# Turning and adding split rows by DMA instead of TensorE and VectorE, in a graph network with a final layer norm

## The reference

```python
x = _layernorm(x + _L0_gnn_ref(x, adj, ...), axis=-1)      # graph convolution, two linear layers, two batch norms
x = _layernorm(x + _L1_gnn_ref(x, adj, ...), axis=-1)
# the last part of _L1_gnn_ref, h is [128 batches, 128 times, 128 channels]:
for p in range(1, 5):
    nw = Tv // p
    wins = h[:, :nw * p, :].reshape(Bv * nw, p, Hd)        # windows of p times
    last = _lstm_last(Wih[p-1], Whh[p-1], bih[p-1], bhh[p-1], wins)   # p steps of an LSTM, the last hidden state
    h = h.at[:, arange(nw) * p + (p - 1), :].set(last.reshape(Bv, nw, Hd))
```

## Time and profile before

| | us |
|---|---|
| median of 3 runs (756.95 to 757.46) | 757.35 |
| the profiled execution | 757.01 |
| its span in the trace | 755.2 |
| TensorE busy | 737.3 (98%) |
| VectorE busy | 657.6 (87%) |
| ScalarE busy | 538.8 (71%) |
| GpSimd busy | 316.5 (42%) |

### The profile page before, as it was taken

One profiled execution on the slowest core, in us unless ns is written; L12 is line 12 of the kernel. 1 busy time (PEld: TensorE's weight loads), 2 busy tenths in 40 slices (PEclk: granted clock), 3 DMA queues, 4 the chain that ended last, 5 costly groups with the idle time before them and its releaser, 6 DMA issues.

```text
span 755.2 us, 11504 instructions
## 1 busy us (share of the span) xinstructions
PE 737.3 (98%) x4016; PEld 426.6 (56%) x4016; DVE 657.6 (87%) x1391; ACT 538.8 (71%) x872; POOL 316.5 (42%) x287
## 2 busy tenths in 40 slices
PE   8999999999999999998999999999999999999994
PEld 6777644677777777673444444444444444554542
DVE  6888787888998989858998799889999898899987
ACT  4877898467777686659887686786676767666662
POOL 1000000159788887800000001600981946239986
PEclk9999999999999999999999999999999999999997
DMA  5642400024424334114300000100000121021012
GB/s 158 189 140 87 112 1 1 1 56 112 112 57 113 83 86 111 30 29 193 141 1 2 0 1 1 43 1 0 28 35 24 38 75 43 1 70 57 15 56 85
DMA packets 64606, 45.08 MB, mean 60 GB/s; under 512 B 1658, under 2 KB 63524, under 8 KB 63524
## 3 DMA queue, kind: packets, MB, share of 16 engines
q1 hardware_dynamic: 64548, 44.33, 19.2%
HBM read 27.55 MB, written 16.78 MB: 59 GB/s over the span
## 4 chain that ended last, share of the span: by engine, by line
PE 53%; DVE 15%; ACT 6%; issue 2%; POOL 1%; DMA 1%; POOLq 0%; DVEq 0%; SPq 0%
PE ps L660 10%; PE ps L661 10%; PE ps L669 10%; PE ps L674 7%; PE ps L665 7%; PE ps L666 7%; ACT work L894 4%; DVE ln_stats L1146 2%; DVE ring L1127 2%; DVE store L1166 2%; DVE ring L1155 2%; DVE work L1110 1%; ACT work L901 1%; DVE work L1096 1%; DVE ring L1160 1%
## 5 line engine op out<-in xcount | busy, mean ns | idle before, releaser
L894 ACT ACTIVATE work<-ps,gate_bias 128x512 f32<-128x512 f32 x449 | 282.6, 680 | 91.1 <-PE ps L674 57.9
L660 PE MATMUL ps<-store,wih 128*128 128x512 f16 (+1 forms) x443 | 166.7, 376 | 2.3 <-ACT work L894 2.3
L661 PE MATMUL ps<-store,wih 128*128 128x512 f16 (+1 forms) x443 | 166.7, 376 | 0.0
L669 PE MATMUL ps<-store,wih 128*128 128x512 f16 (+1 forms) x443 | 156.0, 376 | 0.0
L534 POOL TENSOR_TENSOR end_mv<-end_mv,minus_half 128x12 f32<-128x12 f32 (+1 forms) x16 | 31.0, 1940 | 256.0 <-DVE end_mv L1140 256.0
L525 POOL TENSOR_SCALAR ring<-ring,ln_mv 128x128 f32<-128x128 f32 x112 | 113.3, 1024 | 2.8 <-POOL ln_mv L513 2.7
L1110 DVE TENSOR_TENSOR work<-work 128x512 f32<-128x512 f32 (+1 forms) x129 | 88.2, 684 | 22.5 <-ACT work L901 22.5
L901 ACT ACTIVATE work<-store 128x512 f32<-128x512 f32 x97 | 60.5, 623 | 52.7 <-DVE store L1103 36.2
L665 PE MATMUL ps<-store,whh 128*128 128x512 f16 (+1 forms) x248 | 93.2, 376 | 0.0
L666 PE MATMUL ps<-store,whh 128*128 128x512 f16 (+1 forms) x248 | 93.1, 376 | 0.0
L674 PE MATMUL ps<-store,whh 128*128 128x512 f16 (+1 forms) x248 | 93.0, 376 | 0.0
(11 more groups left out here) (135 smaller groups left out, 1285.8 us busy)
## 6 DMA issues: line engine op xcount, KB each, us to landing
ring<-in_x_dram SPq DMA_DIRECT2D x32, 256.0 KB, 2.9
ring<-in_x_dram SPq DMA_DIRECT2D x16, 512.0 KB, 5.3
x_scratch<-ring SPq DMA_DIRECT2D x16, 512.0 KB, 3.5
ring<-x_scratch SPq DMA_DIRECT2D x5, 1024.0 KB, 4.9
out_dram<-ring SPq DMA_DIRECT2D x5, 768.0 KB, 3.5
store<-x_scratch SPq DMA_DIRECT2D x3, 1024.0 KB, 14.0
out_dram<-store SPq DMA_DIRECT2D x3, 768.0 KB, 3.9
out_dram<-ring SPq DMA_DIRECT2D x5, 256.0 KB, 2.3
```

The source lines that it names most:

```text
L660: nc.tensor.matmul(acc(j), w_hi, x_hi, start=True, stop=False)
L661: nc.tensor.matmul(acc(j), w_lo, x_hi, start=False, stop=False)
L669: last = nc.tensor.matmul(acc(j), weights(wih, j)[0], x_lo, start=False, stop=u.first)
L894: nc.scalar.activation(acts[:, n % 2, gate, 0:u.cols], ps[:, gate_bank(q), 0:u.cols], ACT.Tanh if gate == G else ACT.Sigmoid, bias=gate_bi ...
```

## The change

- `turn_h` and `end_add` remain for row 3 alone. TensorE loses 24 turns, VectorE 24 additions.
- New on SyncE, `move_rows(tile)`: eight transposing DMAs, four per half, from `hist` to a buffer `h_rows` (batches x 12 times x channels, float16, per half). It waits until the low half of the tile's last source unit is there, and until both accumulations of the tile before are complete (`h_added`), since `h_rows` is a single buffer.
- New on GpSimd, `add_rows(tile)`: two accumulating DMAs, high half then low half, that add `h_rows` to three of four rows of x1's tile. Each waits for the four transposes of its half, the second for the first's landing too.
- `ln_slots` plans them: moves one unit after the tile's last source, landings at three, statistics not before seven, and the statistics of rows 0 to 2 now wait for `h_added`. The moments of pieces (tile, 0) come four units later for tile 0, three for tile 6, two for tiles 2 and 7, one for tiles 1 and 4, and as before for 3 and 5. The order of pieces is the same.
- SyncE's list is written by units: a unit's moves, then the output writes of the pieces of four units before.
- `minus_c` and `u1_bias`, used earlier, now lie in the buffer `turned` that `h_rows` takes later.

```diff
@@ -163,8 +163,10 @@
         fixed[NUMBER[Unit(4, tile, 3)] + 1] = tile
     wanted = []
     for tile in range(P // T_TILE):
-        ready = max(NUMBER[v] for v in sources(Unit(4, tile, 0))) + 2
-        wanted.append((max(ready, NUMBER[Unit(4, tile, 0)]), tile))
+        written = max(NUMBER[v] for v in sources(Unit(4, tile, 0)))
+        put(moves, written + 1, tile)
+        put(lands, written + 3, tile)
+        wanted.append((max(written + 7, NUMBER[Unit(4, tile, 0)]), tile))
     places, free = [(at, (tile, 3)) for at, tile in fixed.items()], 0
     for at, tile in sorted(wanted):
         for r in range(3):
...
@@ -174,25 +176,27 @@
             places.append((at, (tile, r)))
             free = at + 1
     for at, piece in sorted(places):
-        put(turns, at, piece)
-        put(adds, at + 1, piece)
+        if piece[1] == 3:
+            put(turns, at, piece)
+        put(stats, at + 1, piece)
         if piece[1] >= 2:
             put(moments, at + 1, (piece[0], 0 if piece[1] == 2 else 3))
-    return turns, adds, moments
-
-
-TURNS, ADDS, MOMENTS = ln_slots()
+    return moves, lands, turns, stats, moments
+
+
+MOVES, LANDS, TURNS, STATS, MOMENTS = ln_slots()
 def in_order(table):
     return [piece for n in sorted(table) for piece in table[n]]
-TURN_ORDER, ADD_ORDER, MOMENT_ORDER = (in_order(t) for t in (TURNS, ADDS, MOMENTS))
+MOVE_ORDER, TURN_ORDER, STAT_ORDER, MOMENT_ORDER = (in_order(t) for t in (MOVES, TURNS, STATS, MOMENTS))
+assert MOVE_ORDER == in_order(LANDS)
+OUT_DELAY = 4
 TAIL = MOMENTS[len(UNITS) - 1]
 N_TAIL = len(TAIL)
 N_POOLED = len(MOMENT_ORDER) - N_TAIL
-assert TURN_ORDER == ADD_ORDER
 def moment_rows(piece):
...
@@ -464,7 +475,20 @@
             sp.wait_ge(gate_done, GATE0[N_EARLY])
             for tile in range(X1_RING):
                 load_x1(tile)
-            for n, piece in enumerate(MOMENT_ORDER):
+
+            def move_rows(tile):
+                n = MOVE_ORDER.index(tile)
+                sp.wait_ge(lo_done, halves_through(max(NUMBER[v] for v in sources(Unit(4, tile, 0)))))
+                wait(sp, h_added, 32 * n)
+                for s in range(2):
+                    for m in range(CB):
+                        t = tile * T_TILE + 4 * m
+                        sp.dma_start(h_rows[:, s, 3 * m:3 * m + 3, :],
+                                     hist[:, s, t:t + 3, :].rearrange("p t b -> p (t b)"),
+                                     transpose=True).then_inc(h_moved[s], 16)
+
+            def write_rows(piece):
+                n = MOMENT_ORDER.index(piece)
                 if n < N_POOLED:
                     sp.wait_ge(end_scaled, n + 1)
                 else:
...
@@ -526,7 +556,17 @@
                                                    ALU.subtract, ALU.mult)
                 last.then_inc(x1_ready, 1)
-            for n, piece in enumerate(MOMENT_ORDER):
+            def add_rows(tile):
+                n = MOVE_ORDER.index(tile)
+                rows = first_rows(x1_tile[tile % X1_RING])
+                pool.wait_ge(x1_loaded[tile % X1_RING], 16 * (tile // X1_RING + 1))
+                for s in range(2):
+                    pool.wait_ge(h_moved[s], 16 * CB * (n + 1))
+                    wait(pool, h_added, 16 * (2 * n + s))
+                    nc.gpsimd.dma_start(rows, h_rows[:, s, :, :].rearrange("p (m r) d -> p m (r d)", r=3), accum_op=ALU.add).then_inc(h_added, 16)
+
+            def scale_rows(piece):
+                n = MOMENT_ORDER.index(piece)
                 tile, rows = piece[0], moment_rows(piece)
                 cols = slice(rows.start * CB, rows.stop * CB)
                 mv = end_mv[:, tile, :, :]
...
@@ -544,6 +584,12 @@
                         last = nc.gpsimd.tensor_scalar(row, row, mv[:, 1, k:k + 1], mv[:, 4, k:k + 1],
                                                        ALU.subtract, ALU.mult)
                 last.then_inc(end_scaled, 1)
+
+            for n in range(N_EARLY, len(UNITS)):
+                for tile in LANDS.get(n, ()):
+                    add_rows(tile)
+                for piece in MOMENTS.get(n, ()):
+                    scale_rows(piece)
         @block.tensor
         def _(pe):
...
@@ -780,23 +826,14 @@
                                                 start=True, stop=True)
                     last.then_inc(gnn_summed, 1)
-            def turn_h(tile, r):
-
-                n = TURN_ORDER.index((tile, r))
+            def turn_h(tile):
+                n = TURN_ORDER.index((tile, 3))
                 last = NUMBER[Unit(4, tile, 3)]
-                if r == 3:
-                    pe.wait_ge(hid_done, last + 1)
-                else:
-                    pe.wait_ge(lo_done, halves_through(max(NUMBER[v] for v in sources(Unit(4, tile, 0)))))
+                pe.wait_ge(hid_done, last + 1)
                 wait(pe, end_added, n - 1)
                 for m in range(CB):
-                    t = tile * T_TILE + 4 * m + r
-                    acc = ps[:, TURN + n % 2, m * P:(m + 1) * P]
-                    if r == 3:
-                        done = nc.tensor.transpose(acc, acts[:, last % 2, O, m * P:(m + 1) * P], ident[:])
-                        continue
-                    nc.tensor.matmul(acc, hist[:, 0, t, :], ident16[:], start=True, stop=False)
-                    done = nc.tensor.matmul(acc, hist[:, 1, t, :], ident16[:], start=False, stop=True)
+                    done = nc.tensor.transpose(ps[:, TURN + n % 2, m * P:(m + 1) * P],
+                                               acts[:, last % 2, O, m * P:(m + 1) * P], ident[:])
                 done.then_inc(h_turned, 1)
             pe.wait_ge(out_stored, CHUNKS)
...
@@ -1177,14 +1214,17 @@
             def end_row_stats(tile, r):
                 rows = x1_tile[tile % X1_RING].rearrange("p (m r) d -> p r m d", r=4)[:, r, :, :]
-                dve.wait_ge(end_added, ADD_ORDER.index((tile, r)) + 1)
+                if r == 3:
+                    dve.wait_ge(end_added, TURN_ORDER.index((tile, r)) + 1)
+                else:
+                    dve.wait_ge(h_added, 32 * (MOVE_ORDER.index(tile) + 1))
                 for m in range(CB):
                     nc.vector.bn_stats(end_stats[:, tile % 2, r, m, :], rows[:, m, :]).then_inc(end_stats_done, 1)
             def end_moments(piece):
                 n = MOMENT_ORDER.index(piece)
                 tile, rows = piece[0], moment_rows(piece)
-                dve.wait_ge(end_stats_done, CB * (ADD_ORDER.index((tile, rows.stop - 1)) + 1))
+                dve.wait_ge(end_stats_done, CB * (STAT_ORDER.index((tile, rows.stop - 1)) + 1))
                 cols = slice(rows.start * CB, rows.stop * CB)
                 moments(end_stats[:, tile % 2, :, :, :].rearrange("p r m s -> p (r m) s")[:, cols, :],
                         end_mv[:, tile, :, cols], end_step, 4 * n, end_var)
```

More of the change, by code:

```diff
@@ L152, in ln_slots @@
 def ln_slots():
-    turns, adds, moments = {}, {}, {}
+    moves, lands, turns, stats, moments = {}, {}, {}, {}, {}
     end = len(UNITS) - 1
@@ L243, in resnorm_gnn_kernel @@
         row_sums = sb("row_sums", [P, P])
-        minus_c = sb("minus_c", [P, CB, P])
-        u1_bias = sb("u1_bias", [P, CB, P])
+        turned = sb("turned", [P, 3 * BANK])
+        minus_c, u1_bias = (turned[:, k * BANK:(k + 1) * BANK].rearrange("p (b n) -> p b n", b=CB) for k in range(2))
+        h_rows = turned[:].bitcast(F16).rearrange("p (s k d) -> p s k d", s=2, d=P)
         wih = sb("wih", [P, 2, NG * P], F16)
@@ L345, in resnorm_gnn_kernel @@
         x1_loaded = [sem(f"x1_loaded{k}") for k in range(X1_RING)]
+        h_moved = [sem(f"h_moved{s}") for s in range(2)]
+        h_added = sem("h_added")
         h_turned, end_added, end_stats_done, end_step, end_var, end_rstd, end_scaled, tail_scaled = (
@@ L398, in unit_cell, with first_rows @@
             return cell_bufs[u.p, u.tile % CELLS[u.p]][:, 0:u.cols]
+        def first_rows(buffer):
+            return buffer.rearrange("p (m r) n -> p m (r n)", r=4)[:, :, 0:3 * P]
         block = ctx.enter_context(nc.Block())
@@ L480, in _ @@
                     load_x1(tile + X1_RING)
+            for n in range(N_EARLY, len(UNITS) + OUT_DELAY):
+                for tile in MOVES.get(n, ()):
+                    move_rows(tile)
+                for piece in MOMENTS.get(n - OUT_DELAY, ()):
+                    write_rows(piece)
             for k in range(X1_RING):
@@ L536, in _ @@
                 if n >= N_POOLED:
-                    continue
+                    return
                 pool.wait_ge(end_step, 4 * (n + 1))
@@ L827, in _ @@
                 lstm_unit(n)
-                for tile, r in TURNS.get(n, ()):
-                    turn_h(tile, r)
+                for tile, _ in TURNS.get(n, ()):
+                    turn_h(tile)
         @block.scalar
@@ L1155, in relu_h0 @@
                 nc.vector.tensor_tensor(h0T[:, h * CB:(h + 1) * CB, :].rearrange("p b n -> p (b n)"), ps[:, H0[h], :],
```

(25 more changed lines are left out.)

1 line of the change is left out of this document (removed).

## The result

The changed kernel takes 768.08 us (median of 4 runs, 767.73 to 768.35) against 757.4 us (756.95 to 757.57): ratio 1.014, 95% interval 1.0128 to 1.0153. That is 10.7 us slower, where 763 us were predicted in a range of 755 to 797. The profiled execution has a span of 765.9 us.

The account below looks back on a forecast made before the run. The prediction took TensorE as the bound up to its last matmul, with the end hanging on GpSimd's queue. Span 754.8 + A 2.9 + B 0 + C 3.3 = 761.0, + 1.8 = 762.8, about 763 us; range 755 to 797.

Parts of the forecast that it names:

- TensorE is the bound and 24 turns are 10.8 us: TensorE, gapless up to its last matmul: 24 turns removed at 0.45 us each save 10.8 us.
- The slots eat the gain through GpSimd's queue: Tiles 6 and 7's later statistics slots on GpSimd's queue leave 0.4 of 10.8 us; span 754.8 with free landings.
- Rival 2: Faster: GpSimd's scalings shorten by 1.6 us without VectorE's 24 additions, time 755.0 if landings are cheap; chance 13%.
- g: GpSimd's issue of one accumulating DMA, taken as 1.2 us.
- d: Time from an accumulating DMA's issue to its landing: 4.9 us taken, 3.5 to 9.8 possible.
- L: Time a tile's landing, two accumulating DMAs, blocks GpSimd: two issues and one landing time, 7.3 us (4.2 to 15.1).
- Term C: GpSimd's late queue: landings 6 and 7 delay its start of piece (6,0) by 3.3 us (0 to 18.9).
- Term A: Tile 2: VectorE's statistics wait 6.6 us for landing 2; beyond 3.7 us of slack it costs 2.9 us (0 to 35).
- T1: Tile 2: time for the first four transposes to be there before the landing's first half, taken as 4.5 us.
- Term B: Tile 4: VectorE's statistics wait 2.3 us for landing 4, inside the slack, so cost 0 (to 12).
- Cheap landings: Landings short enough to cost nothing: span 754.8, time 756.6 us, within 0.2% of no change; chance 15%.
- Slow transposes: A tile's eight transposes run one behind the other at 2.9 us, 23 us together; time 784 us; chance 20%.

Follow-up runs that it names:

- experiment 2: Against the kernel before: rows 0 to 2 neither turned nor added in any tile, statistics in that kernel's old slots; 746.40 us.
- experiment 1: Against the changed kernel: rows 0 to 2 neither turned nor added in any tile, the change's later statistics slots kept; 753.61 us.
- experiment 6: Changed kernel with tiles 6 and 7 back on TensorE in their old slots, six tiles by DMA, one buffer; 760.91 us.
- experiment 10: Changed kernel with tiles 0 to 5 by DMA, two buffers, later statistics for tiles 2 and 4, earlier landings; 749.45 us.
- experiments 7 and 9: Changed kernel with only tiles 0, 1, 3, 4 and 5 by DMA, landings one unit earlier, one buffer; 751.21 and 751.16 us.
- experiment 4: Changed kernel with a second buffer for `h_rows`, so transposes need not wait for the landing of the tile before; 769.1 us.

## Why the prediction was right

**TensorE is the bound and 24 turns are 10.8 us: right.** Experiment 2 gives 10.7, by the medians and by the spans.

**The slots eat the gain through GpSimd's queue: right, and oversized.** The sum had 754.8 of span with free landings, 10.4 above the pure gain; experiment 1 has a span of 751.9, 7.4 above experiment 2's 744.5. I had the last four pieces at their old durations, 43.9 us from (6,0)'s power to (6,3)'s. Experiment 1 needs 42.3 (703.58 to 745.85) and starts 1.0 earlier, the change 39.3. The twelve rows of (7,0) take 12.59 us before, 11.21 in experiment 1 and 9.96 in the change. Rival 2 had such a term (1.6 us), but its reason, that VectorE's additions are gone, does not hold: experiment 2 leaves out the same additions with the old slots, and the scalings of the last four pieces take 35.3 us there against 34.4 before. They are shorter where they come so late that VectorE has little left to do (33.7 us in experiment 1, 31.1 in the change; the last four rows 3.1 instead of 3.7, with VectorE idle).

**Landings: the size was nearly right.** Forecast g 1.2 and d 4.9, L = 7.3, L + d = 12.2. Measured: issue 1.27 to 1.50; L = 7.1 at tile 6 (692.30 to 699.40) and 8.2 at tile 7 (712.33 to 720.55), up to 10.7 at the other tiles; from the second issue to VectorE's start at tile 2, 5.7. The long ones wait for transposes inside the landing. That holds for landing 7 too: its transposes were forecast to be there before GpSimd asks, and GpSimd waited 6.1 us for the second four. Term C, GpSimd's start of (6,0) behind VectorE's readiness: 3.3 forecast. The readiness forecast of 704.6, moved by the 11.65 us of the next point (by which (5,0) comes late as well, 677.18 where 665.5 was forecast), is 716.2 and the start 720.55: 4.3.

**Term A, tile 2: the mechanism and the place right, mis-sized, 2.9 forecast and 11.7 measured.** Its parts, in TensorE's gaps beyond the regular pitch: 7.56 us of stall, 1.6 of half clock in the eight matmuls behind it, 1.4 at 546.4 and 1.0 at 636.7, which is tile 4's (term B). That the sum comes to VectorE's wait of 11.7 us is chance. The step that failed is T1. I took 4.5 us for the first four transposes and nothing for the second four. The profile shows one transpose every 1.36 us (10.90 us for tile 3's eight, with no landing beside them), so the first four took 7.1 us (512.98 to 520.11), and the second four landed 8.7 us later, held up by the first accumulation. That makes the wait 11.7 instead of 6.6. The slack of 3.7 us was right to 0.4 (11.67 - 3.7 = 8.0, against 7.56 measured; experiment 6: 12.14 - 3.7 = 8.4, against 8.03). The clock, which the sum did not have, came on top.

**Term B, tile 4:** 2.3 us of wait forecast, 4.2 measured, 1.0 of it reaching TensorE.

The sum with measured terms: 754.8 + 11.7 (A, with B's gap) + 4.3 (C) - 4.6 (the last four pieces took 39.3 us, 720.55 to 759.82, instead of 43.9) = 766.2, against a span of 765.9. So 763 came from one term 8.8 us too small and one, the duration of GpSimd's rows, 4.6 us too large. That they partly cancel is luck: with the rows as they ran and all else as forecast it would have been 758. The power for (6,3), forecast at about 755 us, came at 759.8.

**Rivals.** Cheap landings: denied by L. Faster: rows do get shorter at the end, but for another reason than it gave, and not by enough. Slow transposes: half true, 10.9 us a tile and not 23. The rule of the Trainium skill (SBUF — State Buffer, "A bandwidth-pool intuition that's wrong"), by which GpSimd's descriptors wait while a VectorE copy holds the shared port, does not show here: all 16 issues took 1.27 to 1.50 us beside a VectorE that is busy for 85% of that stretch. How many of VectorE's operations are of the kind that the rule means, no run here tells.

## What to carry to other kernels

Taking work from the bound engine gives nothing if the new path puts the last pieces later into another engine's in-order queue: before moving a step, follow that queue from the moved piece to the last instruction. Move only what has room, here six of eight tiles, and leave the last ones where they were. By itself that left 0.4% of the loss (experiment 6); with a second buffer and later statistics for two tiles it made 1.4% slower into 1.0% faster (experiment 10), and with five tiles and one buffer into 0.8 to 0.9% faster (experiments 7 and 9). A transfer issued in two dependent DMAs blocks the issuing engine for the first one's round trip, and freeing one chain can let its transfers collide with the next.

## What the runs showed of the hardware

- A transposing DMA of 128 x 384 two-byte elements costs SyncE 1.26 us of issue in the median, one every 1.36 us, against 0.37 for a plain DMA, and lands 2.4 us after its issue. The issues (ns, min, median, max):

```profile
L486 SPq DMA_TRANSPOSE turned<-store x64: 1179/1257/3000, 446.2 to 714.0; - x64
```

and issue to landing (KB, us):

```profile
ring<-turned POOLq DMA_DIRECT2D x10, 768.0 KB, 5.8
...
store<-turned POOLq DMA_DIRECT2D x6, 768.0 KB, 6.0
...
turned<-store SPq DMA_TRANSPOSE x64, 2.4
```

- An accumulating DMA (384 KB of float16 added to 768 KB of float32, both in SBUF): 1.3 us on GpSimd, 5.8 to 6.0 us to landing in the median, up to 9.6 us from issue to the next half's issue in experiment 4.
- GpSimd's row scaling goes with what VectorE does beside it: twelve rows take 16.59 us in one piece and 9.96 in another (1.38 and 0.83 us a row), the long one (2,0) with VectorE busy for 96% of it, the short one (7,0) for 51%. The four rows of (3,3) take 4.94 us in the changed kernel beside a VectorE that is 95% busy, and 3.13 (0.78 a row) in experiment 4, where VectorE stands still for the landing while the DMA engines are at work:

```profile
702.75 3.13 POOL L587 TENSOR_SCALAR store<-store,end_mv 128x128 f32<-128x128 f32 x4 [0.18 <-POOL end_mv L577]
```

- Around 7.4 us of idle time TensorE's clock was at its lower level from 535.0 to 541.8; the eight matmuls that ran in it, in its last 3.4 us, added 1.6 us to the stall. After the stop of 7.9 us in experiment 6 it was 14 matmuls and 2.9 us.
